# Cross attention with a mixture-of-experts FFN: layer norm of the output tiles moved into the projection slots

## The reference

```python
x = x + xattn(layernorm(x), ctx)          # 16 heads of 32
x = x + moe(layernorm(x))
# xattn: q = rms(x Wq + bq) * nq; keys and values of 1344 text and of 257 image rows have their own
# weights; out = (softmax(q kT) v  +  softmax(q kT_img) v_img) Wo + bo
# moe: scores = sigmoid(x Wr); the best 3 of 8 groups, in them the best 4 of 32 experts;
#   each expert takes at most 80 rows, in order of the rows: y = (silu(x Wg) * (x Wu)) Wd, scaled
#   and added to the row; and for all rows, shared: (silu(x Sg) * (x Su)) Sd
```

## Time and profile before

| what | us |
|---|---|
| median of 3 runs | 1437.2 (1431.1 to 1440.23) |
| the profiled execution | 1436.74 |
| its span, first to last instruction | 1435.0 |
| busy: PE, DVE, ACT, POOL | 1250.9, 883.5, 667.3, 183.8 |
| four projections and attentions, to the last attention product | 0 to 936.4 |
| a projection phase with a batch before it | 109 |
| end of attention, norm and router | 936.4 to 1048.9 |
| shared stage with routing | 1048.9 to 1208.9 |
| index and first gather | 1208.9 to 1217.1 |
| experts | 1217.1 to 1435.0 |

### The profile page before, as it was taken

One profiled execution on the slowest core, in us unless ns is written; L12 is line 12 of the kernel. 1 busy time (PEld: TensorE's weight loads), 2 busy tenths in 40 slices (PEclk: granted clock), 3 DMA queues, 4 the chain that ended last, 5 costly groups with the idle time before them and its releaser, 6 DMA issues. The chain is left out here.

```text
span 1435.0 us, 22471 instructions
## 1 busy us (share of the span) xinstructions
PE 1250.9 (87%) x8916; PEld 471.0 (33%) x8916; DVE 883.5 (62%) x1166; ACT 667.3 (47%) x906; POOL 183.8 (13%) x287
## 2 busy tenths in 40 slices
PE   5989998998999899999899899852669896999886
PEld 2442222454222344222245322111534332333332
DVE  5765768875778776676877477753566653222221
ACT  4547885345888244788544588700321111111111
POOL 0110000131000122000013100002400001233332
PEclk9999999999999999999999999976589998999999
DMA  7110001111000211000101000006340201699894
GB/s 282 52 30 9 2 2 67 30 59 31 1 1 2 82 50 54 1 2 2 67 30 60 16 1 2 1 22 251 127 176 0 66 30 49 210 321 303 279 279 120
DMA packets 36035, 113.58 MB, mean 79 GB/s; under 512 B 6241, under 2 KB 6497, under 8 KB 30689
## 3 DMA queue, kind: packets, MB, share of 16 engines
q1 hardware_dynamic: 30816, 101.41, 19.8%
q0 software_dynamic: 5120, 10.82, 3.5%
HBM read 93.57 MB, written 18.63 MB: 78 GB/s over the span
## 5 line engine op out<-in xcount | busy, mean ns | idle before, releaser
L422 ACT ACTIVATE work<-ps 128x1024 f32<-128x1024 f32 (+1 forms) x416 | 403.1, 1021 | 61.1 <-PE ps L857 58.8
L864 PE MATMUL ps<-work,vals 128*32 128x512 f32 (+2 forms) x1792 | 236.7, 604 | 1.0 <-ACT work L422 0.8
L702 PE MATMUL ps<-wts,work 128*128 128x512 f16 x864 | 202.5, 386 | 14.2 <-DVE work L454 14.2
L857 PE MATMUL ps<-quer,keys 32*128 32x512 f16 x2496 | 171.9, 378 | 24.7 <-ACT work L422 9.3
L606 DVE TENSOR_TENSOR work<-work 128x2048 f32<-128x2048 f32 x64 | 146.6, 2291 | 11.4 <-ACT work L422 7.3
L606 DVE TENSOR_TENSOR attn<-attn,work 128x2048 f32<-128x2048 f32 x64 | 146.6, 2290 | 11.2 <-ACT work L422 7.3
L702 PE MATMUL ps<-wts,hl 128*128 128x512 f16 x480 | 112.2, 385 | 20.8 <-DVE hl L454 20.8
L702 PEld LDWEIGHTS ps<-wts,work 128*128 128x128 f16 x864 | 83.5, 99 | 116.6 <-DVE work L454 14.8
L1630 PE MATMUL f_ps<-f_wring,f_x2t 128*80 128x512 f32 x256 | 118.4, 607 | 0.0
L857 PEld LDWEIGHTS ps<-quer,keys 32*128 32x128 f16 x2496 | 46.4, 92 | 214.0 <-ACT work L422 189.1
L1284 ACT ACTIVATE f_x2t<-f_ps,f_wc 80x512 f32<-80x512 f32 x32 | 21.8, 682 | 168.9 <-PE f_ps L1645 153.0
(11 more groups left out here) (186 smaller groups left out, 1440.8 us busy)
## 6 DMA issues: line engine op xcount, KB each, us to landing
f_wring<-in_wx SPq DMA_DIRECT2D x32, 1536.0 KB, 7.6
raw<-in_ctx SPq DMA_DIRECT2D x52, 256.0 KB, 2.7
work<-in_x SPq DMA_DIRECT2D x4, 1024.0 KB, 5.4
work<-in_x SPq DMA_DIRECT2D x16, 256.0 KB, 2.9
x<-work SPq DMA_DIRECT2D x16, 256.0 KB, 2.0
f_x1s<-x SPq DMA_DIRECT2D x4, 1024.0 KB, 9.0
table<-f_xn SPq DMA_DIRECT2D x4, 1024.0 KB, 4.2
out<-f_x1s SPq DMA_DIRECT2D x16, 256.0 KB, 2.3
```

The lines of the kernel that those rows point to most:

```text
L422: act.activation(prob[0:rows, s % PROBS, 2 * half:2 * half + 2, :], ps[0:rows, 2 * pair:2 * pair + 2, :], ACT.Exp, scale=SCALE).then_inc(a ...
L702: mm = pe.matmul(out, lhs(a, c)[:, cols], wts[:, w, z, c * D:(c + 1) * D], start=(k == 0), stop=(k == len(steps) - 1))
L857: mm = pe.matmul(ps[:, 2 * pair + h % 2, :], k[h * HD:(h + 1) * HD, :], q[h * HD:(h + 1) * HD, :], start=(e == 0), stop=(e == len(terms) - 1))
L864: mm = pe.matmul(ps[h * HD:(h + 1) * HD, NUM, :], vals[a:z, ORDER[n], g * P + h * HD:g * P + (h + 1) * HD], prob[a:z, s % PROBS, h, :], st ...
```

## The change

Both programs now share one layout of SBUF (`Memory`), so that buffers of the FFN can be filled while attention runs.

- In `project`, for the batch before: DVE makes `out_stats` right behind `out_rows`, `out_norm` in slots 8, 9, 12, 13 and `norm_low` in slots 9, 10, 13, 14; POOL `out_scale`; ACT `norm_high` and `norm_store`; PE `turn_out` in slots 10, 12, 14, 15. SP stores the normalized rows into the table and the turned rows to DRAM (`x2_dram`).
- During the last attention DVE splits the three shared weights between head groups (`ffn_weight`), and SP loads the turned tiles of batches 0 and 1.
- `last_rows` is gone from the attention program. The FFN program begins with the last batch: four spreads, the router products of 8 tiles, the four output products, one gate-up group, then transposes and the remaining router tiles.
- FFN loops over batches are written out. The copy of the row list and the index stand ahead of gates 14 and 15 and the last down products; gathers wait for `f_gu` and no longer for the last residual. One-hot tiles come in threes.
- In the projection of batch 0 two blocks of zeros are stored. The second pass (not taken) loads its weights again.

```diff
+NORM_SLOT = [8, 9, 12, 13]
+LOW_SLOT = [9, 10, 13, 14]
+TURN_SLOT = [10, 12, 14, 15]
...
         @block.sync
...
-            def residual(bb, b, j):
-                upto(sp, s_st[j % 2], 16 * ((bb * QT + j) // 2))
+            def residual(q, b, j):
+                if j >= 2:
+                    sp.wait_ge(n_norm, xn(q, j - 2))
+                upto(sp, s_st[j % 2], 16 * ((q * QT + j) // 2))
...
+            def store_norm(q, b, j):
+                sp.wait_ge(n_norm, xn(q, j))
+                sp.dma_start(table[b * L + j * P:b * L + (j + 1) * P, 0:D], xn2[j % 2]).then_inc(s_tab[j % 2], 16)
+
+            def store_turned(q, b, j):
+                sp.wait_ge(n_out, xn(q, j))
+                sp.dma_start(x2_dram[b * L + j * P:b * L + (j + 1) * P, :], x2st[j % 2]).then_inc(s_x2[j % 2], 16)
...
                         if b > 0 and i - 1 in O_SLOT:
-                            j = O_SLOT.index(i - 1)
-                            store(bb - 1, b - 1, j)
+                            store(q, b - 1, O_SLOT.index(i - 1))
+                        if b > 0 and i in NORM_SLOT:
+                            j = NORM_SLOT.index(i)
+                            store_norm(q, b - 1, j)
                             if j + 2 < QT:
-                                residual(bb - 1, b - 1, j + 2)
+                                residual(q, b - 1, j + 2)
+                        if b > 0 and i - 1 in TURN_SLOT:
+                            store_turned(q, b - 1, TURN_SLOT.index(i - 1))
...
+                for i in range(3):
+                    sp.dma_start(sstage[i][:, :], d["w3"][i]).then_inc(s_fw[i], 16)
...
+                for t in range(2):
+                    sp.wait_ge(f_wlo, 3 * p + 2 + t)
+                    load_turned(t)
...
         @block.gpsimd
...
+            def out_scale(q, j):
+                pool.wait_ge(n_mv, xn(q, j))
+                pool.tensor_scalar(rs2n, mvn[j % 2][:, 1:2], 1.0, 1e-5, ALU.mult, ALU.add).then_inc(n_var, 1)
...
+                pool.tensor_tensor(rsn[j % 2], rs2n, mhalf, ALU.pow).then_inc(n_rs, 1)
...
         @block.scalar
...
+            def norm_high(q, j):
+                act.wait_ge(n_norm, xn(q, j))
...
+                act.copy(xs2[j % 2][:, 0, :], xn2[j % 2]).then_inc(n_hi, 1)
+
+            def norm_store(q, j):
+                act.wait_ge(n_turn, xn(q, j))
...
+                act.copy(x2st[j % 2], ps[:, 7 - j % 2, :].bitcast(F16)).then_inc(n_out, 1)
...
                     if i in (6, 8, 10, 12):
                         x_store(bb, (i - 6) // 2)
+                    if b > 0 and i in NORM_SLOT:
+                        norm_high(q, NORM_SLOT.index(i))
+                    if b > 0 and i in TURN_SLOT:
+                        norm_store(q, TURN_SLOT.index(i))
...
         @block.vector
...
+            def out_stats(q, j):
+                dve.wait_ge(o_out, xn(q, j))
+                dve.bn_stats(st6n, xres[j % 2]).then_inc(n_st, 1)
...
+                dve.bn_aggr(mvn[j % 2], st6n).then_inc(n_mv, 1)
...
+            def ffn_weight(p, i):
+                dve.wait_ge(s_fw[i], 16 * (p + 1))
+                dve.tensor_scalar(swt[i][:, 0, :], sstage[i][:, :], WS, None, ALU.mult).then_inc(f_whi, 1)
...
+                    if b > 0 and i in NORM_SLOT:
+                        out_norm(q, NORM_SLOT.index(i))
+                    if b > 0 and i in LOW_SLOT:
+                        norm_low(q, LOW_SLOT.index(i))
...
                     if b > 0 and i - 1 in O_SLOT:
-                        out_rows(bb - 1, O_SLOT.index(i - 1))
+                        out_rows(q, O_SLOT.index(i - 1))
+                        out_stats(q, O_SLOT.index(i - 1))
                     key_norm(bb, i)
...
+                    if b == B - 1 and g > 0:
+                        ffn_weight(p, g - 1)
                     dve.wait_ge(a_img, gn(bb, g))
...
-            last_rows(B - 1)
             dve.wait_ge(f_sum, 1)
...
         @block.tensor
...
+                if j == 3:
+                    pe.wait_ge(n_out, xn(q, 0))
...
+                    if b > 0 and i in TURN_SLOT:
+                        turn_out(q, TURN_SLOT.index(i))
                     if b > 0 and i in O_SLOT:
-                        output(bb - 1, O_SLOT.index(i))
+                        output(q, O_SLOT.index(i))
...
-def ffn_program(nc, d, x1_dram, table, out):
+def ffn_program(nc, m, d, x1_dram, x2_dram, table, out):
...
+            for j in range(QT):
+                pool.tensor_tensor(x1t[:, j, :], x1t[:, j, :], vec[:, OB, :], ALU.add).then_inc(t_bias, 1)
...
+            weigh(0)
+            weigh(1)
+            dve.wait_ge(s_r, 32)
+            chain(dve.tensor_scalar(rwt[:, 0, :], rraw[:, :], WS, None, ALU.mult))
...
+            out_low(0)
+            weigh(2)
+            out_low(1)
+            weigh(3)
+            out_low(2)
+            out_low(3)
+            out_rows(0)
+            out_norm(0)
+            norm_low(0)
+            out_rows(1)
+            out_norm(1)
+            norm_low(1)
+            gate(0)
+            gate_low(0)
+            out_rows(2)
+            out_norm(2)
+            norm_low(2)
+            out_rows(3)
+            out_norm(3)
+            norm_low(3)
...
+            for g in range(NG):
+                spread(g)
+            pe.wait_ge(r_lo, 1)
+            pe.wait_ge(t_mt, 1)
+            for j in range(2 * QT):
+                route(j)
+            for j in range(QT):
+                output(j)
+            gate_up(0)
+            turn_out(0)
+            turn_out(1)
+            pe.wait_ge(s_x2, 16)
+            for j in range(2 * QT, 3 * QT):
+                route(j)
+            turn_out(2)
+            turn_out(3)
+            for j in range(3 * QT, NT):
+                rt_last = route(j)
+            rt_last.then_inc(e_r, 1)
...
+            gate_up(12)
+            down(2)
+            for j in (11, 12):
+                slots_of(j)
+            gate_up(13)
+            for j in (13, 14, 15):
+                slots_of(j)
+            gate_up(14)
+            gate_up(15)
+            down(3)
```

More of the change, by code:

```diff
@@ L321, in one_pass @@
                         if b > 0 and i in O_SLOT:
-                            add_bias(bb - 1, O_SLOT.index(i))
-                bb, b = passes(p)[-1]
-                for j in range(QT):
-                    add_bias(bb, j)
+                            add_bias(out_batch(bb - 1), O_SLOT.index(i))
+                        if b > 0 and i - 1 in O_SLOT:
+                            out_scale(out_batch(bb - 1), O_SLOT.index(i - 1))
             one_pass(0)
@@ L915, in attention @@
                 denominator(NG - 1, 0, sums[(NG - 1) % 2], P, last=True).then_inc(a_den, 1)
-            def last_rows(bb):
-                for g in range(NG):
-                    spread(bb, g)
-                for j in range(QT):
-                    output(bb, j)
             def one_pass(p):
@@ new lines, in _ @@
+            norm_high(1)
+            gate_tanh(0)
+            norm_store(0)
+            gate_high(0)
+            norm_high(2)
+            norm_store(1)
+            norm_high(3)
+            norm_store(2)
+            norm_store(3)
+            act.wait_ge(e_r, 1)
+            act.activation(rt[0][:, :, :].rearrange("p j e -> p (j e)"), ps[:, ROUTER, :], ACT.Exp,
+                           scale=-1.0 / WS).then_inc(e_ez, 1)
+            for n in range(1, 14):
+                gate_tanh(n)
+                gate_high(n)
@@ L1274, in _ @@
             cp.then_inc(e_ar, 1)
+            for n in range(14, 4 * NI):
+                gate_tanh(n)
+                gate_high(n)
             def expert(n, u):
@@ new lines, in out_low, with out_rows @@
+            def out_low(g):
+                dve.wait_ge(t_hi, g + 1)
+                TT(attn[:, g, 1, :], nums[:, g, 0, :], attn[:, g, 0, :], ALU.subtract).then_inc(t_lo, 1)
+            def out_rows(j):
+                dve.wait_ge(t_mm, j + 1)
+                dve.wait_ge(t_bias, j + 1)
+                dve.scalar_tensor_tensor(x1t[:, j, :], ps[:, OUT_BANK[j], :], 1.0 / WS, x1t[:, j, :], ALU.mult,
+                                         ALU.add).then_inc(t_out, 1)
+                dve.wait_ge(t_out, j + 1)
+                chain(dve.bn_stats(st6, x1t[:, j, :]))
+                dve.bn_aggr(mv[j], st6).then_inc(n_mv, 1)
@@ L1575, in _, with spread, output @@
-            pe.drain().then_inc(e_r, 1)
-            def slots_of(j, half):
+            def spread(g):
+                image, text = SEL_BANK[g]
+                pe.matmul(ps[:, image, :], sel[:, g, 1, :], rcp[:, :], start=True, stop=True)
+                pe.matmul(ps[:, text, :], sel[:, g, 0, :], rcp[:, :], start=True, stop=True).then_inc(t_sel, 1)
+            def output(j):
+                if j == 0:
+                    pe.wait_ge(t_lo, NG)
+                if j == 3:
+                    pe.wait_ge(t_out, 1)
+                product(ps[:, OUT_BANK[j], :], lambda a, c: attn[:, c, a, j * P:(j + 1) * P],
```

(1 more changed line is left out.)

1023 lines of the change are left out of this document (520 added, 503 removed).

## The result

The changed kernel takes **1397.3 us** (median of 4 runs, 1396.3 to 1397.7), beside 1438.7 for the kernel before in the same comparison: a ratio of 0.972, 95% interval 0.968 to 0.976. A second comparison of the same program gave 1395.1 and 0.972 (0.968 to 0.976). The forecast was 1396, the range 1374 to 1419.

A forecast was written before the change was run, and what follows sets the result against it. PE, busy 87%, plus its gaps, the largest 112.5 us before the FFN; DVE's loop in projection, POOL's scatters in experts. From 1436.7 us, +22, -53, 0, -8, -2 sum to -41: 1396 us, range 1374 to 1419.

The forecast's parts named there:

- A, projection: Norm of 12 output tiles in projection slots: 7.4 us a phase, with 2.1 for ACT's order and 0.8 taken off; +22.
- B, shared weights: Splitting shared weights between head groups of the last attention hides in VectorE's 4.30 us idle: nothing, 0.1 a group at worst.
- C, transition: From last attention to FFN gate-up: reading x1 back and norm of 12 tiles removed, 59.3 us against 112.5, -53.
- The clock under the outputs: Last batch's output products, behind router products, priced at 12.2 us with half-clock start, not 10.4; the skill's warm start, 2 less.
- D: Shared products: stalls ahead of down(2) and the position product go, one-hot and late-gate waits come; 0, ends -6 and +6.
- E: Index ahead of the last gates removes PE's idle before the first expert, -8; first expert at full clock, -2.
- F: Expert stage: same scatter chain and same ring, 0.
- 1: Projection is PE's: DVE's additions vanish in its lead, only 5.4 is paid; 1379, chance 0.22.
- 2, the burst: New program's 11.5 MB load burst delays a table store, or its code comes late; some 10 lost, 1406, chance 0.15.
- 3: DVE and ACT additions in the projection exposed whole, 44 in three phases; 1418, chance 0.05.
- 4: A projection tile's chain is exposed link by link, 7.7 a tile, 92 for twelve; 1466, chance 0.04.
- 5: Transition's work isn't really taken out, the last batch's chain takes as long; about 1430, chance 0.04.

The follow-up runs named there:

- moving the store: Changed kernel with ScalarE storing each turned tile one slot later, behind the next key's cast instead of ahead of it; 1389.7 us.
- late adds: Changed kernel with GpSimd's index tables written behind the last low half and the last batch's bias adds moved there, each ahead of its row; 1393.2 us.
- tripled transposes: Changed kernel with each normed tile's transposes in the projection issued three times over, 24 instead of 8; 1398.2 us.

## Why the prediction was right, step by step

- **A, projection (+22; +19.8).** Right in mechanism: DVE's queue carries it, 2.0 of the statistics' 3.5 us vanish in its wait for POOL (10.4 to 8.4), norm and low part are paid. The 7.4 us a phase stand against 6.6 measured. Oversized was ACT's 2.1: DVE's waits for its cast rose by 0.3 (11.3 to 11.6), and moving the store gained nothing. The 0.8 taken off was a misreading: DVE waited for PE elsewhere too, and its wait for the transposed keys rose from 0.7 to 2.0 while the 0.8 fell to 0.5.
- **B, shared weights (0; 0).** The scaling took 1.22 (bound: 2.1) and lies in the wait for PE, which went from 4.30 to 0.84.
- **C, transition (-53; -53.5), partly by luck.** The text put 64.5 us from the last reciprocal to the next gate-up, 64.15 came, made up of other parts. The router products took 2.7, not 7.5 (28 ns each), and were not on the path: they waited for the router's split on DVE, and DVE's weighing let the outputs begin 29.1 us after the reciprocal, where the text had 30.0 (966.5 - 936.5). With late adds they begin at 26.7, so the weighing had been given 1.8 too much (28.5), and the adds beside it cost 2.5: the text had the right rows for POOL's port and left that "2.5" out of the sum. From the outputs' start 35.0 stand against 34.5: the table write beside the last norm, 2.3, was not seen, the outputs took 0.3 more, and the other steps had been given about 2.1 too much. The costs left out and the costs set too high happened to be equal.
- **The clock under the outputs** was given 12.2; it was 12.71, and 12.73 without router products ahead. The granted clock was 0.59 from 979 to 982, while 96 router products ran, and 0.50 from 982 to 985, while PE waited. With late adds it read 1.00 during the router products and 0.66 from 982 to 987, where the outputs start, and these took 12.21, still 1.7 above the 10.52 of 48 products at full clock. The Trainium skill, "TensorE: Matmul & The Clock Gate", Part 4, names transposes alone as not counting as PE being busy. By it the outputs could have started warm; in none of these kernels did they. The windows (length, busy of PE, PEld, DVE, ACT, POOL, granted clock, DMA share, GB/s) of the changed kernel:

```profile
979.00:982.00 3.00, 2.37 (x91) 2.27 (x87) 2.90 (x6) 0.62 (x1) 0.00 (x0) 0.59 1.05 386
982.00:985.00 3.00, 0.00 (x0) 0.00 (x0) 2.81 (x5) 0.62 (x1) 0.00 (x0) 0.50 1.10 414
```

and of the one with late adds:

```profile
976.00:979.00 3.00, 3.00 (x98) 2.55 (x96) 2.90 (x5) 0.50 (x2) 0.00 (x0) 1.00 1.05 402
...
982.00:987.00 5.00, 4.33 (x13) 1.66 (x14) 0.62 (x1) 0.00 (x0) 4.23 (x5) 0.66 1.06 424
```

- **D (0; +4.1)** held in work and failed in waits. The stalls ahead of the third down products and of the position product went, as forecast (2.56 and 1.85 us). But the one-hot waits were four of 1.15 where three of 1 were priced, 0.73 came ahead of a gate-up group, and the wait ahead of the last down products rose by 1.0 and those ahead of the first two by 0.9 together. That is 2.7 us more of waits, and 1.3 of slow clock with them. It was within the ±6.
- **E (-10; -11.4)** as said, and the first expert's 3.2 instead of 2 is the clock's: it meets a warm PE.
- **F (0; +0.5)**, the same chain, 6.30 to 6.31.
- **Rivals.** 1 fell with the tripled transposes; 2, the burst: DVE never waits for a table store in the new program; 3 and 4 would have needed phases 15 and 31 us longer, against 6.6; 5 is refuted by C.

## What to carry to other kernels

An engine that is 94% busy, as PE in these phases, may still be the one with room: ask which engine's idle rows name the other, then test by adding work, as the tripled transposes did, and look at the clock beside it, which the added work may raise. POOL's idle time is no gift while DVE works on SBUF: place POOL's long operations under DVE's waits or its PSUM reads. And end a stage's waits for two reasons, the wait and the clock behind it; but judge such an edit over the whole span, since the next stage may give it back.

## What the hardware showed that I had not expected

- POOL holds up DVE operations with one SBUF source too: 0.55 became 1.48 beside an add and 2.87 beside a 2.66 us table write, and 0.22 became 1.29; DVE operations that read PSUM kept their 0.68 beside the same adds. The Trainium skill, "GPSIMD Engine Reference", section 1, names DVE instructions in a two-port performance mode beside those with two SBUF inputs. The trace agrees for two SBUF inputs, and shows operations with one held up as well; in which mode they ran it doesn't show. The prediction used only the second kind.
- Router products of 32 columns hardly feel the clock: 96 took 2.68 us at 0.59 and 2.56 at 1.00.
- The clock's answer to a wait was the same to 0.02 us in both profiled executions of the changed kernel, and differs by up to 3 us between programs at the same wait; one of that kernel's eight runs had another mean clock, so the repetition isn't complete.
